# A routed feed-forward kernel: router for two tiles at a time, compact state products, and a third causal mask on VectorE

## What is computed

```
x = layernorm(X)
Q = rms_norm_per_head(x Wq^T), V = rms_norm_per_head(x Wv^T), K = x      16 heads of 16
W_t = sum over s <= t of K_s V_s^T   per head and batch (16 x 16)
X2 = X + Q_t W_t                                                           linear attention
u = layernorm(X2)
scores = softmax(u Wg)                                                     32 experts
y = sum over the 4 best experts of score * swiglu(u, W1, W3, W2)
z = swiglu(u, Ws1, Ws3, Ws2)                                               shared expert
out = X2 + y + z
```

## Time and profile before

| | |
|---|---|
| median of 3 runs | 577.72 us (577.47 to 579.74) |
| the profiled execution: its own time | 579.97 us |
| its span, first to last instruction | 578.2 us |
| PE, DVE, ACT, POOL busy in the span | 554.6, 374.4, 384.1, 350.0 us |
| attention and router loop, its regular part | from 45 to 211 us |
| experts begin | 271.09 us |

### The profile page before, as it was taken

One profiled execution on the slowest core, in us unless ns is written; L12 is line 12 of the kernel. 1 busy time (PEld: TensorE's weight loads), 2 busy tenths in 40 slices (PEclk: granted clock), 3 DMA queues, 4 the chain that ended last, 5 costly groups with the idle time before them and its releaser, 6 DMA issues.

```text
span 578.2 us, 16242 instructions
## 1 busy us (share of the span) xinstructions
PE 554.6 (96%) x4041; PEld 392.7 (68%) x4041; DVE 374.4 (65%) x1417; ACT 384.1 (66%) x1322; POOL 350.0 (61%) x399
## 2 busy tenths in 40 slices
PE   6899999999999998799999999999999999879997
PEld 3466667666667666456888888888888885444654
DVE  6688999999999998574333333333333335762787
ACT  2689999999999996321566666666666665662543
POOL 5123777777777777660455555555555554456992
PEclk8999999999999999989999999999999999999999
DMA  8998555445555444773677776666666654438998
GB/s 254 315 280 272 187 198 198 177 176 209 193 190 209 174 173 176 243 287 92 179 216 215 216 212 183 183 181 186 185 186 171 187 172 151 125 106 329 409 409 315
DMA packets 65080, 123.16 MB, mean 213 GB/s; under 512 B 9824, under 2 KB 44000, under 8 KB 64992
## 3 DMA queue, kind: packets, MB, share of 16 engines
q1 hardware_dynamic: 47824, 78.07, 42.8%
q0 software_dynamic: 13056, 39.86, 19.1%
q10 hardware_dynamic: 4112, 4.19, 2.1%
HBM read 58.49 MB, written 63.60 MB: 211 GB/s over the span
## 4 chain that ended last, share of the span: by engine, by line
PE 84%; DVE 5%; issue 3%; ACT 3%; DMA 1%; POOL 1%; SPq 1%; ACTq 0%; DVEq 0%; POOLq 0%
PE pS L936 19%; PE pS L952 9%; PE pQV L838 9%; PE pS L722 9%; PE pS L762 5%; PE pO L859 5%; PE pQV L918 3%; PE pT L918 3%; PE pO L819 3%; PE pT L802 2%; PE pQV L738 2%; PE pO L738 2%; PE pT L791 2%; PE pT L749 2%; PE pT L773 2%
## 5 line engine op out<-in xcount | busy, mean ns | idle before, releaser
L484 POOL DMA_INDIRECT ys<-gsh,dst x144 | 138.0, 958 | 124.1 <-ACT gsh L645 102.9
L456 POOL DMA_INDIRECT xs<-xg,posi x128 | 123.6, 966 | 52.7 <-issue 26.2
L936 PE MATMUL pS<-w,after_a 128*128 x512 | 132.5, 381 | 0.0
L936 PEld LDWEIGHTS pS<-w,after_a 128*128 128x128 f32 x512 | 87.2, 190 | 7.5 <-issue 0.2
L952 PE MATMUL pS<-w,after_a 128*128 x256 | 76.6, 381 | 0.0
L644 ACT CAST dst<-xg 128x1 int32 x128 | 24.5, 191 | 77.0 <-PE pS L952 76.1
L1281 DVE COPY after_a<-pT 128x128 f32<-128x128 f32 x72 | 21.0, 292 | 68.2 <-PE pT L941 67.0
L1281 DVE COPY after_a<-pO 128x128 f32<-128x128 f32 x72 | 21.0, 291 | 67.3 <-PE pO L941 67.1
L838 PE MATMUL pQV<-w 128*128 128x512 f32 x128 | 62.0, 608 | 0.5 <-ACT w L563 0.5
L645 ACT ACTIVATE gsh<-pS,xg 128x256 f32<-128x256 f32 x128 | 60.6, 473 | 0.4 <-issue 0.4
L472 POOL TENSOR_SCALAR_AFFINE_SELECT w<-w 128x512 f32<-128x512 f32 x64 | 39.3, 640 | 30.0 <-ACT w L517 29.6
(11 more groups left out here) (209 smaller groups left out, 1183.9 us busy)
## 6 DMA issues: line engine op xcount, KB each, us to landing
xg<-xs SPq DMA_DIRECT2D x128, 160.0 KB, 2.5
ys<-gsh SPq DMA_DIRECT2D x32, 512.0 KB
w<-ys SPq DMA_DIRECT2D x32, 512.0 KB, 15.2
w<-in_L_ffn_W ACTq DMA_DIRECT2D x1, 4096.0 KB, 18.5
out<-xall SPq DMA_DIRECT2D x14, 256.0 KB, 6.1
xs<-padrow SPq DMA_DIRECT2D x32, 80.0 KB
xg<-xs SPq DMA_DIRECT2D x32, 80.0 KB, 2.7
ys<-gsh,dst POOLq DMA_INDIRECT x144
```

The source lines that it names most:

```text
L456: pool.indirect_dma_start(out=xs, out_offset=bass.IndirectOffsetOnAxis(ap=posi[:, a.r8, k:k + 1], axis=0), in_=xr[:, a.r8, :], in_offset=N ...
L484: pool.indirect_dma_start(out=ys, out_offset=bass.IndirectOffsetOnAxis(ap=dst[:, j % 8:j % 8 + 1], axis=0), in_=y[:, j % 8, :], in_offset= ...
L936: last = pe.matmul(pS[a.b][:, 0:2 * F], xgT[:, a.b, k, :], w13_of(e, k), start=(k == 0), stop=(k == KC - 1))
```

## The change

1. **Router for pairs of tiles.** `closing(tile)` is the tile if its number is odd. Router operations run once for two tiles, on 64 columns, where the operation allows it: logits, their copy, maximum negation, `v8`, mask, reciprocal, probabilities (now `tensor_tensor` with the reciprocal broadcast), rank products and their copy, rank times mask, positions. Those that work on one list (largest eight, replacement, exponential, running count, destinations) stay once for each tile. Router ages rise by one or two steps, to 7, 8 and 9; the indirect transfers go from age 7 to age 9, still four for each tile.
2. **Logits transposed in column groups.** `Wg` is the stationary operand, and the tokens move: four products for a pair, each 32 partitions high. ACT copies the result to `lgT`, and a product with `pick`, a 0/1 matrix, adds the two halves of the contraction and transposes back.
3. **Compact state.** The state product and o1 are eight products each with 32 columns of stationary data, in place of two 128x128 ones; DVE spreads the result with a broadcast (`tensor_tensor` of the same 256 elements). Both stand right in front of the attention product.
4. **A third mask on DVE.** DVE masks banks 0, 3 and 2; ACT copies and POOL masks bank 1 only.
5. **Order.** The step's order is rewritten on all four engines. xnT follows x2T on PE and has its own half of bank pT0; `qT` has two buffers. DVE puts router work between the three Newton operations. Seven, not six, products of the shared expert stand in front of `cnt`.

```
 PE
-                    for k in range(KC):
-                        last = pe.matmul(pT0[:, D:D + E], x2T_all[:, k, a.t * P:(a.t + 1) * P], wg[:, k, :],
+                    for h in range(2):
+                        for k in range(KC):
+                            j = KC * h + k
+                            last = pe.matmul(pT0[32 * j:32 * j + 32, 0:P], wg[:, k, :],
+                                             x2T_all[:, k, (a.t - 1 + h) * P:(a.t + h) * P], start=True, stop=True,
...
+                if (a := closing(tile_of(6))) is not None:
+                    wait(pe, S["lgT_done"], a.p + 1)
+                    wait(pe, S["qm_done"], a.t + 6, NT)
+                    pe.matmul(pT0[:, P:P + 2 * E], lgT[:], pick, start=True, stop=True).then_inc(S["logits_ps"], 1)
...
-                    for g in range(KC):
-                        last = pe.matmul(pT1[:, g * P:(g + 1) * P], xn[:, a.r3, g * P:(g + 1) * P],
-                                         vp[:, a.b, 4 * g:4 * g + 4, 0:3:2, :], start=(a.t % NTB == 0 and g == 0), stop=True,
+                    for g in range(KC):
+                        for j in range(4):
+                            last = pe.matmul(pT1[32 * j:32 * j + 32, g * 2 * d:(g + 1) * 2 * d],
+                                             xn[:, a.r3, g * P + 32 * j:g * P + 32 * j + 32], vp[:, a.b, 4 * g + j, 0:3:2, :],
...
-                        last = pe.matmul(pO[:, g * P:(g + 1) * P], w_bd[:, a.b, g * P:(g + 1) * P], qT[:, g, :],
+                        for j in range(4):
+                            at = g * P + 32 * j
+                            last = pe.matmul(pO[32 * j:32 * j + 32, g * P:(g + 1) * P], w_bd[:, a.b, at:at + 32], qT[:, a.b, g, :],
 POOL
-                if (a := tile_of(7)) is not None:
+                if (a := tile_of(9)) is not None:
                     pool_wait(S["xr_done"], a.t + 1)
-                    pool_wait(S["prob_done"], a.t + 1)
+                    pool_wait(S["prob_done"], a.p + 1)
...
                 if (a := tile_of(2)) is not None:
-                    for n, j in enumerate((1, 0)):
-                        pool_wait(S["s_copied"], 2 * a.t + n + 1)
+                    pool_wait(S["s_copied"], banks_copied(a.t) + 1)
+                    v = s_sb[:, 1].rearrange("p g r l -> p (g r) l")
 DVE
+                if (a := closing(tile_of(8))) is not None:
+                    wait(dve, S["rin_done"], a.p + 1)
+                    dve.tensor_tensor(xr[:, a.r8 - 1:a.r8 + 1, D:D + E], ex[:, a.pb], rin[:].unsqueeze(2).to_broadcast([P, 2, E]),
+                                      ALU.mult).then_inc(S["prob_done"], 1)
...
+                if (a := tile_of(3)) is not None:
+                    mask_scores(a, 0)
...
+                if (a := tile_of(3)) is not None:
+                    mask_scores(a, 3)
...
+                if (a := tile_of(3)) is not None:
+                    mask_scores(a, 2)
...
+                        dve.tensor_tensor(w_bd[:, 1 - a.b, :].rearrange("p (g j c) -> p g j c", g=KC, j=4),
+                                          pT1[:, 0:KC * 2 * d].rearrange("p (g c) -> p g c", g=KC).unsqueeze(2).to_broadcast([P, KC, 4, 2 * d]),
+                                          head_mask[:].rearrange("p g (j c) -> p g j c", j=4), ALU.mult).then_inc(S["state_done"], 1)
```

More of the change, by code:

```diff
@@ L47, in pipelined, with closing @@
         step(tile_of)
+def closing(tile):
+    return tile if tile is not None and tile.t % 2 else None
 def wait(eng, sem, count, most=None):
@@ L543, in step @@
[L543 to L580, removed]
-                        for g in range(KC):
-                            last = act.activation(qm[:, r, g, :], pT0[:, g * P:(g + 1) * P], ACT.Copy,
-                                                  scale=mwq[:, r, g:g + 1])
-                    last.then_inc(S["qm_done"], 1)
@@ L595, in step @@
-                if (a := tile_of(6)) is not None:
-                    wait(act, S["rank_ps"], a.t + 1)
-                    wait(act, S["vm_done"], a.t)
-                    act.copy(rk[:], pT0[:, D + E:D + 2 * E]).then_inc(S["rk_done"], 1)
-            pipelined(NT, 7, step)
+            pipelined(NT, 8, step)
             act.preload_act_table(ACT.Silu)
@@ new lines, in step @@
+                if (a := tile_of(2)) is not None and a.t < NT - 1:
+                    wait(pe, S["v_done"], a.t + 1)
+                    wait(pe, S["state_done"], a.t)
+                    for g in range(KC):
+                        for j in range(4):
+                            last = pe.matmul(pT1[32 * j:32 * j + 32, g * 2 * d:(g + 1) * 2 * d],
+                                             xn[:, a.r3, g * P + 32 * j:g * P + 32 * j + 32], vp[:, a.b, 4 * g + j, 0:3:2, :],
+                                             start=(a.t % NTB == 0 and g == 0), stop=True, skip_group_check=True)
+                    last.then_inc(S["state_ps"], 1)
@@ L1031, in _ @@
             dve.wait_ge(S["wc_in"], 64)
+            dve.wait_ge(S["ident_done"], 2)
+            halves = ident[:].rearrange("p (h k e) -> p h k e", h=2, k=KC)
+            chain(dve.tensor_tensor(pick.rearrange("p (h e) -> p h e", h=2), halves[:, :, 0, :], halves[:, :, 1, :], ALU.add))
             for r in range(2):
@@ new lines, in step @@
+                if (a := closing(tile_of(8))) is not None:
+                    wait(dve, S["mask_done"], a.p + 1)
+                    wait(dve, S["mcum_done"], 2 * a.p)
+                    wait(dve, S["rank_ps"], a.p - 1)
+                    dve.tensor_tensor(mcum[:, a.pb, 1, :], mcum[:, a.pb, 0, :], mask[:, a.pb, 0, :], ALU.add
+                                      ).then_inc(S["mcum_done"], 1)
+                if (a := tile_of(3)) is not None:
+                    mask_scores(a, 3)
+                if (a := tile_of(4)) is not None:
+                    wait(dve, S["x2_done"], a.t + 1)
+                    dve.bn_stats(st2[:], xall[:, a.t, :]).then_inc(S["stats2"], 1)
@@ L1173, in half_gate @@
+            pipelined(NT, 9, step)
             def half_gate(g, m):
```

461 lines of the change are left out of this document (273 added, 188 removed).

## The result

The changed kernel takes 570.43 us (median of 4 runs, 569.73 to 570.52) where the kernel before takes 578.3 beside it: a ratio of 0.9838, 95% interval 0.9807 to 0.9869. The forecast was 569.7 in a range of 563.5 to 577.5. The profiled execution took 570.52 us with a span of 568.8; before it was 579.97 and 578.2. On two of the four chips that the experiments met, the kernel before takes as long as here. On the other two it takes 632 and 644 us; the changed kernel was run on the second of them and is 6.6% slower there.

A forecast was written before the change was run, and what follows sets the result against it. PE was taken to set the pace, DVE 0.15 us a step behind. Loop -10.9, POOL +1.9 and slow start +1.0 made -8.0: profiled 579.97 to 572.0, the median 2.25 lower at 569.7 us, range 563.5 to 577.5.

The forecast's parts named there:

- State: State product on PE in the loop of attention and router: from 0.45 us to 16 narrow records, 0.43 us.
- Other terms on PE: PE's remaining pieces of a loop step, such as scores 1.07, QV 1.72, o1 0.43; all of PE together 6.20 us.
- Router per pair: Router products on PE for two tiles: logits 0.22, `pick` 0.25, rank 0.20; 0.67 us a pair, 0.34 a tile.
- Period: One step of the attention and router loop: 6.30 us, 0.35 less than before, worth 8.8 us over 25 steps.
- DVE: DVE's busy time per loop step: savings of 0.90 against 0.60 for the third mask, so 6.50 becomes about 6.2 us.
- the optimistic end of its bounds: DVE per loop step if all savings come and POOL never holds it up: 6.0 us; the other bound was 6.9.
- POOL's hold-up: POOL's mask can make a DVE operation in the loop wait: 0.24 us once a pair, putting DVE at 6.3.
- The rival in which DVE becomes the limit and the kernel slower: In the loop, DVE at its upper bound of 6.9 us a step: kernel at 585.9 us; chance 0.10.
- POOL's transfers: Behind the loop: 30 transfers after the last mask instead of 22, 37.8 us, 8.6 more; 1.9 of the gain lost.
- three terms: From last transfer to experts: transfer landing 2.5, load landing 2.5, slower loads at first 1.0; 6.0 us.
- The slow start: At the experts' start, the granted clock falls in PE's idle time before them: 1.0 us lost.
- The sum: Whole kernel: -10.9 for the loop, +1.9 for POOL, +1.0 for the slow start, -8.0 us in all.

The follow-up runs named there:

- pe_more: Changed kernel with one more 128x128 product on PE behind QV in each step: 571.72 us, 0.9852 of the kernel before.
- dve_two: Changed kernel with two more 128x256 products on DVE in front of its first mask in each step: 585.93 us, 1.0107 of the kernel before.
- late_pads: Changed kernel with the stores of padding rows beginning at block load 16, not the first: 686.33 us, 1.0667 of the kernel before on that chip.
- both: late_pads with four 512-column products without use in front of the experts: 691.65 us, 1.0763 of the kernel before on that chip.
- after_again: The changed kernel unedited, run again on another chip: 683.3 us, 1.0658 of the kernel before there.
- full_state: Changed kernel with the state product and o1 over the full array again, two products each: 675.03 us, 1.0673 of the kernel before there.
- mask_alone: Kernel before with bank 0 masked by DVE instead of copied by ACT and masked by POOL, nothing else: 620.38 us, 0.98 of the kernel before there.

## Why the prediction was right, point by point

**State: mis-sized.** The forecast took the attention product's 0.027 a record and came to 0.43 for sixteen; they take 0.12, 7.5 ns each. These records move 32 columns, those of the attention product 128, and a quarter of 0.027 is 7 ns: between these two widths the price goes with the columns. The lower bound given there, 0.020, was too high. The floor of some 60 cycles that the Trainium skill states (TensorEngine Tiling, Performance Considerations, Instruction Overhead), by estimate 0.025 us at 2.4 GHz, does not add up over products that lie side by side: the trace shows less than a third of it a record. Counted by group it could still hold, since four groups side by side make 0.03 us a record in each; no run has a narrower product that would tell. The mis-sized state product is 0.31 us of step.

**Other terms on PE: right in sum.** o1 was put at 0.43 and takes 0.44 or 0.57; scores and x2T came as written. The attention product was put at 1.03 and takes 0.88 or 0.93. Router per pair: 0.36 + 0.22 + 0.17 to 0.21, up to 0.79, for 0.67. QV takes 1.8 to 1.9 where 1.72 was carried over. Altogether the forecast was 6.20 and the chain has 6.12. It fits better than it deserves, and that is luck: the state's 0.31 too much offset 0.2 too little elsewhere; and pe_more shows that pieces of this chain are not prices.

**Period: forecast 6.30, it is 6.1 to 6.17.** I had added 0.1 because three nearly equal limits never fit exactly. They do fit, to 0.1 us: PE 12.21, DVE 12.01 of 12.22 in a pair. The rule of thumb was the term that was too large here, and it is worth 25 x 0.13 = 3.3 of the 4.6 us by which the end of attention came earlier than forecast (15.5 for 10.9).

**DVE: 6.2 forecast, 6.0 measured** (12.01 a pair), the optimistic end of its bounds. Most of the difference is `v8` and positions. They take 0.30 and 0.35 for each tile before (L1073, L1070) and 0.14 and 0.16 for a pair after (L1175, L1210), so they fell to less than the half that the forecast took. The probabilities (L1153) take 0.22 a pair. POOL's hold-up is well seen in the kernel before: L1136 takes 0.48 to 0.52 us in all 20 steps in which it meets a mask of POOL and 0.24 in 11 of the 12 others. After, none of the 16 operations of L1153 stands beside a mask, so the forecast's doubt about it was not put to the test. The same rows also bear on who set the pace before: from 183 us on L1136 takes 0.24, and the steps are 6.64 (184.73 to 211.27) instead of 6.65: DVE had 0.24 us less to do and the step kept its length, so DVE was not the limit there. The rival in which DVE becomes the limit and the kernel slower did not come about, but it was near: with 0.67 us more on DVE a step, dve_two lies at 1.01.

**POOL's transfers: right in mechanism, and confirmed one for one.** 30 transfers behind the last mask take 38.3 us (213.80 to 252.05), 37.8 forecast. From their end to the experts it is 4.6 us, where 6.0 was put together from three terms. So the loss at PE's start of the experts was 1.1 instead of 1.9.

**The slow start: under-priced.** One microsecond was put on it; it was 3.3. PE's timeline, two rows of after, then the same two of before:
```profile
259.28 1.91 PE L965 MATMUL pS<-w,after_a 128*128 x4
...
263.18 0.42 PE L970 MATMUL pT<-ident,after_a 128*128 128x128 f32 x1
```
```profile
272.10 1.13 PE L936 MATMUL pS<-w,after_a 128*128 x4
...
274.15 0.27 PE L941 MATMUL pT<-ident,after_a 128*128 128x128 f32 x1
```
From the first transposes to the first hidden product it is 2.6 us after (256.69 to 259.28) and 1.0 before; PE stands 1.60 for its second load in it. That is 1.6 of the 3.3. The next stretch, the same products, takes 3.9 against 2.05 with PE busy all the time; the granted clock of 0.63 shown above accounts for these 1.85. The rest of the way to the first scattered result is 0.1 shorter than before. SP issues its first two loads 2.0 us apart in both kernels, with a store of padding between them; but before, the first one leaves 7.1 us in front of the first transposes (264.01), after only 2.2 (254.45). What PE would gain by stores that come later stays untested: late_pads and both were run only where PE is held.

**The sum.** Forecast -10.9 + 1.9 + 1.0 = -8.0; measured in the span -15.5 + 1.1 + 3.3 + 1.7 = -9.4. The gain in the loop was larger than forecast, and so was the part given back. That 569.7 lies so near to the median of 570.43 is in part luck: the profiled execution of before was 2.25 above the median that the forecast started from, and that difference was carried over, while the one of after is 0.1 above its own.

**What the prediction did not hold at all** is the chip on which it would be run. The rival "slower" was DVE's. On chip 15 the change is slower by another mechanism, in which PE is held, and so are its three variants on chip 13.

What starts a hold is not settled. The runs show this: they begin at the ninth or tenth step, with the loop in full, in all seven kernels of the changed form; they come about once in 18 us; the experts, where PE is busy for 98% (88.2 of the 90 us from 380 on in after_again), run at a granted clock of 1.00 and lose 9 us, not 89. The number of products doesn't order the kernels: full_state has 4037, after_again 4793, and they are at 1.067 and 1.066. mask_alone has the 4041 of before, a PE that rests 9% of the time and no half clock in the loop, and is the fastest there; its pauses come in every second step as well, but last 1 us and not 6. The shorter pauses agree with theory T, that PE is held after a long stretch without rest. But the experts, with a PE that rests only 2%, are not held, and mask_alone, with 9%, is: rest alone doesn't order them. The test of T was dve_two, and that ran on an undisturbed chip. So T is argued, not shown. No trace shows before on a chip where it takes over 620 us, so what it loses there, and why mask_alone loses less, stays open as well, and slower supply of instructions inside the loop isn't excluded.

## What to carry to other kernels

When the transfers that an engine issues are moved to a later age, count what stands behind the last one of the loop: two tiles here, 8 transfers, and it became the critical path one for one. A busy share of 100% on PE is no proof that PE sets the pace; add a small known piece to PE and another to the engine behind it, and compare the slopes, before a term is priced from the chain. And measure a gain of 1 to 2% on several chips: this one is 0.984 on one and 1.066 on another.

## What the hardware showed unexpectedly

- Products in column groups with 32 moving columns cost 7.5 ns each (16 in 0.12 us), with 128 moving columns 27 ns (32 in 0.88).
- The same small VectorE operation took 0.48 to 0.52 us in all 20 steps in which it met a mask of GpSimd, and 0.24 in 11 of the 12 others (L1136 of before).
- One product of 128x128 more on PE a step, 0.22 us in its own row, lengthened the step by 0.04 us in the pair shown and 0.07 over 25 steps; the product of another type behind it fell from 0.19 to 0.03.
- On two of the four chips of the experiments PE is held in the loop: groups of three to five products, 0.3 us pauses, about 6 us every second step, and a granted clock of 0.56 in the 6 us behind (levels of 2.4 and 1.2 GHz). The kernel before takes 632 and 644 there, not 578; the changed one takes 683 on the second.
- A kernel whose PE rests for 9% of the loop (mask_alone) kept a granted clock of 1.00 there, was held for 1 us instead of 6 every second step, and was 2% faster than before.
